# 273 score units move their exponential to VectorE, value batches follow a plan, and guests and normalisation change places

## What is computed

```python
h = tok(x)                                        # 4 x 3137 x 128
q, k, v = layernorm(h) @ Wq, @ Wk, @ Wv           # 8 heads of 16
attn = softmax(q k^T / 4 + pos_bias)              # 4 x 8 x 3137 x 3137
h = h + (attn v) @ Wo
y = layernorm(h)
gates = softmax(pool(y) @ gate_w + gate_b); top 2 of 8
h = h + sum over the two experts e of g_e * gelu(gelu(y @ w1[e] + b1) @ w2[e] + b2)
```

## Time and profile before

| | us |
|---|---|
| median of 3 runs | 2862.59 (2859.88 to 2864.08) |
| the profiled execution, its own time | 2861.5 |
| its span | 2859.8 |
| ACT busy in the span | 2564.2 |
| PE busy | 2547.9 |
| DVE busy | 846.0 |
| POOL busy | 786.6 |
| the 2167 exponentials of L846 (busy) | 2246.4 |

### The profile page before, as it was taken

How to read it: one execution, slowest core, us unless ns; L and a number is a source line. 1 busy time by engine, 2 the same in 40 slices (tenths; PEclk the granted TensorE clock), 3 DMA queues, 4 the chain that set the end, 5 groups by cost and what they waited for, 6 DMA issues and landing times.

```text
span 2859.8 us, 121986 instructions
## 1 busy us (share of the span) xinstructions
PE 2547.9 (89%) x55860; PEld 1222.0 (43%) x55860; DVE 846.0 (30%) x1246; ACT 2564.2 (90%) x2733; POOL 786.6 (28%) x1424
## 2 busy tenths in 40 slices
PE   7988888888889999888899898889999988999997
PEld 3443333333344444433444444334444433455554
DVE  4760111111114233311243343112433421244410
ACT  4769999999999999999999999999999999744553
POOL 2112333333333333333333333332333333100000
PEclk8989999999999999999999999999999999999998
DMA  5550001111111100011111000101110000300010
GB/s 129 176 174 7 29 30 32 32 32 32 33 42 35 35 30 30 30 47 33 42 36 35 30 30 29 49 32 40 35 35 29 29 29 31 127 26 29 15 35 19
DMA packets 65897, 125.31 MB, mean 44 GB/s; under 512 B 10034, under 2 KB 55180, under 8 KB 63892
## 3 DMA queue, kind: packets, MB, share of 16 engines
q1 hardware_dynamic: 63324, 110.93, 12.2%
q0 software_dynamic: 2048, 6.43, 0.6%
HBM read 67.30 MB, written 51.30 MB: 41 GB/s over the span
## 4 chain that ended last, share of the span: by engine, by line
ACT 51%; PE 26%; issue 19%; DMA 2%; DVE 1%; POOL 0%; SPq 0%; ACTq 0%; POOLq 0%
ACT shared L846 50%; PE ps L714 6%; PE ps L722 6%; PE ps L750 5%; PE ps L671 3%; PE ps L668 2%; PE ps L698 1%; DMA k_halves<-halves 1%; PE ps L612 1%; PE ps L606 1%; PE ps L627 0%; DMA band_rows<-band_sb 0%; DVE std L968 0%; POOL ln L915 0%; PE ps L620 0%
## 5 line engine op out<-in xcount | busy, mean ns | idle before, releaser
L846 ACT ACTIVATE shared<-ps 128x1179 f32<-128x1179 f32 x2167 | 2246.4, 1302 | 5.9 <-PE ps L671 4.3
L750 PE MATMUL ps<-shared,va 64*32 64x393 f32 x25600 | 1573.1, 499 | 1.1 <-issue 0.8
L929 POOL TENSOR_TENSOR shared<-shared,e_all 128x310 f32<-128x310 f32 (+19 forms) x1344 | 728.5, 554 | 1539.5 <-ACT shared L846 1533.0
L671 PE MATMUL ps<-qa,ka 48*32 48x393 f16 (+2 forms) x15200 | 728.1, 319 | 149.9 <-ACT shared L846 149.0
L668 PE MATMUL ps<-qa,ka 51*32 51x393 f16 (+8 forms) x13184 | 655.9, 314 | 104.3 <-ACT shared L846 103.8
L750 PEld LDWEIGHTS ps<-shared,va 64*32 64x32 f32 x25600 | 620.3, 139 | 28.9 <-issue 4.5
L671 PEld LDWEIGHTS ps<-qa,ka 48*32 48x32 f16 x15200 | 229.8, 90 | 630.9 <-ACT shared L846 619.7
L668 PEld LDWEIGHTS ps<-qa,ka 51*32 51x32 f16 x13184 | 205.8, 89 | 660.6 <-ACT shared L846 658.7
L1006 DVE COPY xc<-ps 128x393 f32<-128x393 f32 x64 | 36.4, 568 | 1102.6 <-PE ps L750 1102.5
L865 ACT ACTIVATE qa<-ps,b 128x393 f32<-128x393 f32 x256 | 136.4, 585 | 85.0 <-PE ps L714 84.9
L1014 DVE RECIPROCAL sq<-sq 128x393 f32<-128x393 f32 x64 | 167.3, 2615 | 2.2
(11 more groups left out here) (143 smaller groups left out, 1320.7 us busy)
## 6 DMA issues: line engine op xcount, KB each, us to landing
qa<-q_halves SPq DMA_DIRECT2D x64, 196.5 KB
ka<-k_halves SPq DMA_DIRECT2D x64, 196.5 KB
att_rows<-std SPq DMA_DIRECT2D x64, 196.5 KB, 3.4
v_rows<-v_sb SPq DMA_DIRECT2D x4, 1600.0 KB, 6.9
va<-v_rows SPq DMA_DIRECT2D x32, 200.0 KB, 15.9
ln_rows<-ln SPq DMA_DIRECT2D x32, 196.5 KB, 5.6
q_halves<-halves SPq DMA_DIRECT2D x32, 196.5 KB, 3.1
k_halves<-halves SPq DMA_DIRECT2D x32, 196.5 KB, 4.2
```

The costliest lines, as they stand in the source:

```text
L671: last = nc.tensor.matmul(out[x:y, cut:W], ka[r:r + 48, par, k0 + x:k0 + y], qa[r:r + 48, par, q0 + cut:q0 + W], start=True, stop=True, ti ...
L750: last = nc.tensor.matmul(ps[quad:quad + 32, O_PS + half, 0:W], va[r:r + 64, par, :, kt], pr[r:r + 64, g % SLOTS_PR, j], start=(kt == 0), ...
L846: nc.scalar.activation(pr[:, g % SLOTS_PR, 0:m], ps[:, b0:b0 + m, 0:W], ACT.Exp, scale=1.0 / (LIFT * LIFT)).then_inc(s_exp, 1)
L929: nc.gpsimd.tensor_tensor(p, p, e_all[0:keys, n % HEADS, t:t + z - a], ALU.mult).then_inc(s_biased, 1)
```

## The change

1. *Exponential on DVE.* `fast_order` also returns `d_at`: 273 groups whose third unit is not part of ACT's exponential. In 21 passes without guests there are five of them, wanted at positions 24, 38, 52, 66 and 80; in the 42 passes with guests four, at 24, 41, 55 and 72. A wanted place slips until the third unit is one without a band. For such a group ACT's operation covers two banks (786 columns), and DVE computes the third unit in nine operations (`exponential`). PE's scores of group g + 2 wait for the first of them (`s_d_read`), the batch that holds the unit waits for the last (`s_d_exp`). A factor LOG2E is folded into Wq and the bias, and taken out again in ACT's scale.
2. *Value batches in a planned order.* A list `turns`, made at build time, says which batch follows which group: a batch with a DVE unit is due seven groups after it (`D_LAG`), others four. The first and the last batch of a pass keep their places. A batch starts with its upper half of rows when the last score unit used the lower half.
3. *Normalisation by loaded chunk.* `drain` keeps only the two operations that add the O banks, and SP stores the sums without normalisation. `load_attention` also loads the denominators (a second DMA for each chunk), and `normalise` on DVE takes the reciprocal and multiplies, once for each of the 32 chunks, at position 17 of the pass in which guest Y of the chunk stands; in the last stage, two expert units ahead of it. 64 reciprocals become 32, and the 64 shuffles are gone.
4. *Guests at other places.* `guest_plan` replaces `guest_order`: positions 37, 68 and 86, V only at 86, and in the list each V is directly followed by the S of its chunk. The last stage uses the same list.

```diff
-def guest_order():
+def guest_plan():
+    seen = {"Y": 0, "M": 0, "V": 0, "S": 0}
+    plan = []
+    for p in range(1, 2 * HEADS):
+        y_here = False
+        for pos in (37, 68, 86):
+            if pos == 86:
+                kinds = [("V", "M")]
+            else:
+                kinds = [("S", "V"), ("M", "Y"), ("Y", None)]
...
+    return plan + [("G", 0, 15, 37)]
 def fast_order(B, KT):
...
+    busy = {q // PASS for q in places}
+    wanted = [q * PASS + pos for q in range(1, 2 * NBH) for pos in ((24, 41, 55, 72) if q in busy else (24, 38, 52, 66, 80))]
...
+        elif len(d_at) < len(wanted) and u >= wanted[len(d_at)] and u + 2 < len(units) and plain(u + 2):
+            d_at[len(groups)] = len(d_at)
...
+            turns, made = [], set()
+            g = 0
+            while len(made) < NB:
+                room = 0 if g in guest_at else 1
+                turn = []
+                while True:
+                    q = min(m for m in range(NB) if m not in made) // KT if len(made) < NB else NB
+                    due = [m for m in range(q * KT, min(q * KT + KT, NB)) if m not in made]
+                    ready = [m for m in due
+                             if max(group_of[u] + (D_LAG if u in d_unit else DELAY + AHEAD) for u in batches[m]) + (m % KT == 0) <= g
+                             and (m % KT < KT - 1 or len(due) == 1) and (m % KT == 0 or q * KT in made)]
...
 def scores(g):
+    if g - AHEAD in d_at:
+        pe.wait_ge(s_d_read, d_at[g - AHEAD] + 1)
...
 def values(m, upper_first):
+    for u in batches[m]:
+        if u in d_unit:
+            pe.wait_ge(s_d_exp, d_unit[u] + 1)
...
-                    m = len(groups[g])
+                    m = len(groups[g]) - (g in d_at)
...
 def drain(q):
+    dve.wait_ge(s_o_out[side], at(16 * (q // 2)))
...
-    nc.vector.tensor_copy(tick[:, 0:1], o_sb[:, side, 0:1]).then_inc(s_tick, 1)
-    nc.vector.stream_shuffle(inv[:, side], o_sb[:, side], [HD + i % HD for i in range(32)]).then_inc(s_shuf, 1)
-    nc.vector.reciprocal(inv[:, side], inv[:, side]).then_inc(s_inv, 1)
-    nc.vector.tensor_tensor(o_norm[:, side], o_sb[:, side], inv[:, side], ALU.mult).then_inc(s_norm_o, 1)
+def normalise(b, c):
+    dve.wait_ge(s_att[c % 4], 32 * (b * CH // 4 + c // 4 + 1))
+    nc.vector.reciprocal(den[c % 4], den[c % 4]).then_inc(s_den, 1)
+    dve.wait_ge(s_den, b * CH + c + 1)
+    nc.vector.tensor_tensor(att[:, c % 4], att[:, c % 4], den[c % 4], ALU.mult).then_inc(s_norm_att, 1)
+def exponential(k):
+    g = d_group[k]
+    x, whole, p = root[:, 0], root[:, 1], root[:, 2]
+    dve.wait_ge(s_score, g + 1)
+    nc.vector.tensor_scalar(x, ps[:, GMAX * (g % 2) + 2, 0:W], -0.25 / (LIFT * LIFT), EXP2_OFFSET, ALU.mult, ALU.add).then_inc(s_d_read, 1)
+    dve.wait_ge(s_d_read, k + 1)
+    nc.vector.tensor_scalar(whole, x, ROUND, None, ALU.add).then_inc(s_d_step, 1)
+    dve.wait_ge(s_d_step, k * D_STEPS + 1)
+    nc.vector.scalar_tensor_tensor(x, whole, ROUND, x, ALU.subtract, ALU.subtract).then_inc(s_d_step, 1)
+    dve.wait_ge(s_d_step, k * D_STEPS + 2)
+    nc.vector.scalar_tensor_tensor(p, x, EXP2[4], x, ALU.add, ALU.mult).then_inc(s_d_step, 1)
+    nc.vector.tensor_scalar(whole.bitcast(I32), whole.bitcast(I32), 23, EXP_BITS,
+                            ALU.logical_shift_left, ALU.bitwise_xor).then_inc(s_d_step, 1)
+    for i in range(3):
+        dve.wait_ge(s_d_step, k * D_STEPS + 4 + i)
+        nc.vector.scalar_tensor_tensor(p, p, EXP2[3 - i], x, ALU.add, ALU.mult).then_inc(s_d_step, 1)
+    dve.wait_ge(s_d_step, k * D_STEPS + 7)
...
+    nc.vector.scalar_tensor_tensor(pr[:, g % SLOTS_PR, 2], p, EXP2[0], whole, ALU.add, ALU.mult).then_inc(s_d_exp, 1)
...
     for g in range(NG + 4):
+        if g in d_at:
+            exponential(d_at[g])
         if g in guest_at:
             receive(guest_at[g], GMAX * (g % 2) + 2)
         if g in drain_at:
             drain(drain_at[g])
+        if g in normalise_at:
+            normalise(*normalise_at[g])
```

More of the change, by code:

```diff
@@ L81, in score_groups @@
     return groups + tail
-def guest_order():
-    steps = []
-    for s in range(CH + 3):
-        for kind, lag in (("Y", 0), ("M", 1), ("V", 2), ("S", 3)):
-            if 0 <= s - lag < CH:
-                steps.append((kind, s - lag))
-    return steps + [("G", 0)]
+def guest_plan():
[8 more added lines that the diff above has]
+                kinds = [("S", "V"), ("M", "Y"), ("Y", None)]
+            for kind, after in kinds:
+                c = seen[kind]
+                if c < CH and (after is None or c < seen[after]) and not (kind == "Y" and y_here):
+                    seen[kind] += 1
+                    y_here = y_here or kind == "Y"
+                    plan.append((kind, c, p, pos))
+                    break
+    assert len(plan) == 4 * CH and plan[-1][2] <= 13
+    return plan + [("G", 0, 15, 37)]
 def fast_order(B, KT):
@@ L98, in fast_order, with plain @@
     units = [(n, kt, 4 * side + c) for n in range(NBH) for side in range(2) for kt in range(KT) for c in range(4)]
-    places = []
-    for b in range(B - 1):
-        q = 2 * HEADS * (b + 1)
-        places += [(q + 1 + i // 3) * PASS + (35, 58, 80)[i % 3] for i in range(4 * CH)] + [(q + 14) * PASS + 58]
-    groups, guest_at, u = [], {}, 0
+    plan = guest_plan()
+    places = [(2 * HEADS * (b + 1) + p) * PASS + pos for b in range(B - 1) for kind, c, p, pos in plan]
+    busy = {q // PASS for q in places}
+    wanted = [q * PASS + pos for q in range(1, 2 * NBH) for pos in ((24, 41, 55, 72) if q in busy else (24, 38, 52, 66, 80))]
+    def plain(u):
+        n, kt, c = units[u]
+        lo = kt * P - REACH
+        return kt < KT - 1 and max(lo, c * (-(-((KT - 1) * P + 65) // CH)), 0) >= min(lo + BAND, (c + 1) * (-(-((KT - 1) * P + 65) // CH)))
+    groups, guest_at, d_at, u = [], {}, {}, 0
     while u < len(units):
@@ L112, in fast_order @@
     batches = [list(range(m, m + 4)) for m in range(0, len(units), 4)]
-    return units, groups, batches, guest_at
+    return units, groups, batches, guest_at, d_at
 def build(nc, B, S, d):
@@ L376, in build @@
             GATE_OPS = 15
-            guest_list = guest_order()
+            guest_list = [(kind, c) for kind, c, p, pos in guest_plan()]
+            chunk_pass = {c: p for kind, c, p, pos in guest_plan() if kind == "Y"}
             def guest(k):
@@ L398, in build @@
             DELAY = 2
-            units, groups, batches, guest_at = fast_order(B, KT)
+            units, groups, batches, guest_at, d_at = fast_order(B, KT)
+            assert T == (KT - 1) * P + 65
             NG = len(groups)
@@ L560, in _ @@
                         load_attention(b, 6)
+                    if b >= 0 and into == 3:
                         load_attention(b, 7)
@@ L738, in values @@
                         pe.wait_ge(s_vld[par], (n // 2 + 1) * 16)
-                    for half in range(2):
+                    for half in (1, 0) if upper_first and 0 < kt < KT - 1 else (0, 1):
                         r = 64 * half
@@ L754, in values @@
                     last.then_inc(s_pv, 1)
-                done = 0
-                for g in range(NG + DELAY + AHEAD):
+                for g in range(len(turns)):
                     if g < NG:
                         scores(g)
-                    turn = 1
                     if g in guest_at:
                         visit(guest_at[g], GMAX * (g % 2) + 2)
-                        turn = 0
-                    while done < NB:
-                        lag = g - group_of[batches[done][-1]] - (done % KT == 0)
-                        if lag < DELAY + AHEAD or (turn == 0 and lag < HOLD):
-                            break
-                        values(done)
-                        done += 1
-                        turn = 0
-                while done < NB:
-                    values(done)
-                    done += 1
+                    for m in turns[g]:
+                        values(m, g < NG and groups[g][-1] % 2 == 0)
                 pe.wait_ge(s_exp, NG)
```

64 lines of the change are left out of this document (43 added, 21 removed).

## The result

The changed kernel takes 3040.02 us (median of 4 runs, 3022.97 to 3045.99), the kernel before 2861.24 (4 runs, 2856.34 to 2864.08). The ratio is 1.0619 (95%: 1.0581 to 1.0658): slower by 6%, 145 us beyond the forecast of 2895 and 80 beyond the range's upper end. The profiled execution of after is the fastest of its four, 3022.97 us for a span of 3021.3. What follows divides its 161.5 us over before's profiled execution; the other 17 us between it and the median are not divided.

The account below looks back on a forecast made before the run. Attention was taken as bound by ACT's rate, with PE fully busy in the last stage. 2861.5 - 91 (ACT) + 103 (late DVE) + 20 (last stage) = 2893.5, against the median 2895 us; range 2810 to 2960.

Parts of the forecast that it names:

- carried lateness: Attention: DVE works in order, so lateness passes on; a read 0.9 us late, a guest's about 0.4, costs nothing.
- ACT's gain: Attention: each unit moved off ACT saves 0.33 us, 273 units 91 us, if PE and DVE keep up.
- I take 5.2, the middle rounded up: DVE in attention: time per unit taken as 5.2 us, between 4.8 and 5.5.
- the upper end: DVE in attention: a unit takes 5.5 us when its operations are lengthened by POOL's work.
- the lower end: DVE in attention: the nine operations take 4.8 us from one unit to the next.
- steep in the length of a unit: Attention: gains 53 us with units of 4.8 us, loses 73 with 5.5.
- its addition: Attention: lateness summed over passes, 44 us in the 21 without guests and 59 in the 42 with guests.
- What leaves DVE: worth 0: DVE: fewer drain operations and 32 normalisations give free time where it was not late, worth 0.
- Batches waiting for a unit: Attention: value batches seven groups after a unit cost 0, or 0.1 to 0.5 us each if band-half units exceed 5.6.
- The last stage: Last stage: S waits for V's chain and PE stands still 2.45 us for each of eight chunks, +20 us.
- the second: Rival 2, attention: POOL stretches every unit to 5.5 us, 2955 us in all; chance 0.19.
- Half of each pass has no band: Attention: argument against rival 2, that POOL has no band to work on in half of each pass.

Follow-up runs that it names:

- e3b: Changed kernel with DVE units of two operations instead of nine, the polynomial left out: 2817.41 us, ratio 0.9867.
- e4: Changed kernel with POOL's band multiplication cut to 8 columns, the rest of the band not applied: 2853.63 us, ratio 0.9982.
- e6: Changed kernel with only the 139 DVE units outside the half of a pass in which POOL multiplies the band: 2862.19 us, ratio 1.0019.
- e7: Changed kernel with only the 134 DVE units inside the half of a pass in which POOL multiplies the band: 3009.71 us, ratio 1.0546.
- e9: Changed kernel with no unit on DVE and guest V at position 80 instead of 86 in odd passes: 2888.00 us, ratio 1.0114.
- e10: Changed kernel with POOL's band cut to 8 columns and two more DVE operations in each of the 134 band-half units: 2996.22 us, ratio 1.0485.
- e5: Changed kernel with 231 DVE units further apart and the last image's guests in the sequence of before: 2937.60 us, ratio 1.0283.
- e1: Changed kernel with no unit on DVE, all other parts of the change kept: 2900.18 us, ratio 1.0152.
- e2: Changed kernel with the guests of the last image in the sequence of before: 3012.54 us, ratio 1.0547.

## Why the prediction was wrong

The direction and the mechanism of carried lateness were right. The size of the losses was not (103 us forecast, 218 measured), and a term put at nothing cost 17. Step by step:

**ACT's gain, 0.33 us a unit: right.** e3b measures 0.30, with whatever its short units still cost. In pass 4 the exponential of a group with a quiet unit is followed by the next after 0.76 us, of which 0.70 were forecast.

**"I take 5.2, the middle rounded up": this step failed.** The 273 units of after take 5.57 us on average, more than the 5.5 that was given as the upper end. A unit in the quiet half takes 4.9 to 5.1 us (e4, e6), so the lower end, 4.8, was right within 0.1 for the quiet half; but one in the band's half takes 6.2 (e7). The upper end was too low because it took the means of operations that met POOL only in part; in the band's half POOL is at work during most of a unit, and one-input operations in SBUF suffer too (0.36 to 0.48 us on average at L1083, 1.01 in pass 4). The trace shows where the 0.69 us between 4.88 and 5.57 come from: an operation of DVE that starts while one of POOL is under way doesn't end before that one has ended (the section on the hardware). The middle of 4.9 and 6.2 is 5.55, not 5.2. And "steep in the length of a unit" was the prediction's own warning: its addition, which gave 103 us of losses for 5.2, gives 179 for 5.57, and 180 with 4.88 in the quiet half and 6.2 in the other. That is 77 of the 115 us by which the measured losses, 218, exceed the forecast's. The addition with lengths from the runs (for after those of e4 and e7; in after itself the two halves take 5.05 and 6.11, which changes it by about 2 us), beside what was measured:

| kernel | lengths, us | addition | measured loss |
|---|---|---|---|
| e4_narrow_band | 4.88 all | 49 | 46 (62 against e9) |
| e6_quiet_half | 5.07 | 9 | 8 |
| e10_narrow_long | 4.88 and 6.1 | 170 | 183 (199 against e9) |
| after | 4.88 and 6.2 | 180 | 218 |
| e7_band_half | 6.19 | 99 | 153 |
| e5_spread | 4.88 and 6.2 | 57 | 148 |

For e4 and e10 the figure against e9 is the fair one. So the rule of carried lateness, with its allowance of 0.9 us for a unit and 0.4 for a guest, holds within 1 us in e6 and gives about four fifths of the loss in e4, e10 and after; in e7 it gives two thirds and in e5 well under half.

**What the addition does not give, 38 us in after.** In passes without guests it is nearly right (69 against 73 measured), in those with guests it falls short (about 111 against 145). Three things can be in it, and no run parts them. The lengths scatter, up to 7.2 us: with each unit's own length the addition gives about 14 us more in after. POOL lengthens the guests' chains too; but without it, in e10, the addition falls short in the passes with guests as well (104 against 128 over e9's), so that is the smaller part. And the clock, which the prediction left out: attention in the trace of after has 171 us at half clock, before's 21, e1's and e4's 42 and 40. ACT's gaps inside those stretches add up to 56 us in after and 12 in e1, but most of such a gap is the wait that the addition already counts. In e7 and e5 the addition is short by 54 and 91 us; with each unit's own measured length in it, it still gives only 112 and 63. Their half-clock stretches are 145 and 115 us long, and what e5's drains find on DVE is not in the addition. That a wait of 2 to 3 us costs more than its length is shown in pass 4; how much of the 54 and 91 us it explains stays open.

**"What leaves DVE: worth 0"; guests at other places.** Priced at nothing, they cost 17 us: in odd passes V at 86 keeps DVE for 9.7 us, with POOL at work, and the drain of the pass comes to stand behind it (e1, e9); at 7.0 us, in even passes and in e4, it costs nothing. The prediction had both lengths of the chain, but looked at what the units and the normalisations find on DVE, not at what the drain finds there. Normalisation, planned order and second DMA are worth 0 as forecast: with V moved, e9's attention is before's within 1 us.

**Batches waiting for a unit.** Forecast at 0, or 0.1 to 0.5 us each for units over 5.6. In after some 18 batches started within 0.12 us of a unit's last operation, but the trace puts no idle time of PE down to that operation, nor to the band. What they cost was not measured; it is inside the losses.

**The last stage: +20 forecast, +25 measured, +27 against e2.** PE waits for L1140 eight times, 18.5 us in all and up to 2.4 each, as forecast. The rest against e2, 8 us, is in part the clock behind four of the waits, at most 5 us.

**The sum again.** 2861.5 - 91 + 218 + 17 + 25 = 3030.5; less 8 us by which the first exponential starts earlier (203.1 instead of 211.0), 3022.5 against 3022.97. It closes because the 218 are a remainder, what attention lacks after the other terms, and so it proves none of them. Against the forecast's 2893.5 that is 129 more: 77 by the length of the units, 38 beyond the addition, 17 at the drains, 5 in the last stage, less the 8. Of the rivals, the second named what happened, POOL on the units. "Half of each pass has no band" was no argument against it: half the units at 6.2 bring the mean above the rival's 5.5.

The Trainium skill, "GPSIMD Engine Reference", Specifications, says that GpSimd shares its SBUF interfaces with VectorE and that they contend for instructions with two SBUF inputs or in a two-port mode. The trace agrees: without POOL's bands L1087 takes 573 ns and L1083 359, with them 681 and 481, and in e10, where POOL has 31 us of work in 200, 572 and 359.

## What to carry to other kernels

When work moves to an engine that another one can hold up, price it where the other is busy and where it is not, apart, and put the units where it is not (139 in the quiet half save 38 us of attention, 134 in the other cost 109). Ask of every wait of PE what clock it leaves behind. When an operation is moved, look at what stands behind it in its new place, the drain above all, and how long its own work takes there, not only at what stands in front.

## What the runs showed of the hardware

- DVE and POOL slow each other. The nine operations of a unit, 393 columns each, take 4.88 us without POOL's bands and 6.19 in the band's half (up to 7.2), single two-input ones 0.57 and up to 1.24. POOL's own multiply of 310 columns goes from 812 to 884 ns, all its bands from a mean of 554 to 665. This is the row of after:

```profile
L981 POOL TENSOR_TENSOR shared<-shared,e_all 128x310 f32<-128x310 f32 x160 | 141.4, 884 | 89.3 <-ACT shared L898 87.6
```

- DVE waits for the end of POOL's operation. The units of after have 1638 operations with two inputs in SBUF. 448 of them took over 0.65 us; in all 448 an operation of POOL was under way at the start, and 435 of them ended 0.42 to 0.43 us after it did, the others later. The 137 lengthened one-input operations in SBUF (L1078, L1083) ended 0.22 us after POOL's. The read of PSUM (L1076) met POOL in 110 units and took 0.55 to 0.57 us in each. Two places in the timeline of after:

```profile
359.07 0.99 POOL L981 TENSOR_TENSOR shared<-shared,e_all 128x201 f32<-128x201 f32 x1 [0.30 <-ACT shared L898]
...
359.63 0.85 DVE L1082 SCALAR_TENSOR_TENSOR root<-root 128x393 f32<-128x393 f32 x1
...
363.32 0.92 POOL L981 TENSOR_TENSOR shared<-shared,e_all 128x192 f32<-128x192 f32 x1
363.83 0.85 DVE L1091 SCALAR_TENSOR_TENSOR shared<-root 128x393 f32<-128x393 f32 x1
```

POOL's end at 360.06 and 364.24, DVE's at 360.48 and 364.68.

- TensorE's granted clock fell from 1.00 to 0.50 behind some waits of 2.3 to 2.6 us, and matmuls took 0.89 instead of 0.52 us (pass 4) and up to 1.68 instead of 0.93 (last stage) there. It did not fall behind each: of the eight waits of one length in the last stage four had a fall close behind them, of the 33 waits of 2 us or more in attention 16.
